# A two-layer kernel on one Trainium2 core: layer 0's start, with x staged in halves around w_out, one pass for bias and column sums, batch 1's statistics taken earlier, and chunk 0's last steps moved

## The reference, cut to what matters

```python
xs = in_proj_w @ gn(x)                       # 768 -> 1536 channels
xs = silu(depthwise_conv3x3(xs) + conv_b)
dt, Bs, Cs = split(x_proj_w @ xs)            # 48 + 4 + 4 rows
delta = softplus(dt_w @ dt + dt_b)
h[t] = exp(delta*A)*h[t-1] + delta*u*Bs      # scan over 4096 tokens, 4 states
y = sum_n(h*Cs) + D*u
y = layernorm(y over 1536 channels)*ln_g + ln_b
x = x + out_proj_w @ y                       # 1536 -> 768 channels
```

## Time and profile before

| what | value |
|---|---|
| time of the profiled execution | 3577.93 us |
| its span | 3576.1 us, so 1.8 us lie around it |
| median of three runs | 3577.36 us |
| busy shares of the span | TensorE 94%, VectorE 80%, ScalarE 67%, GpSimd 66% |
| VectorE busy in 60 to 80 us | 2.94 of 20 us |
| VectorE busy in 160 to 180 us | 12.46 of 20 us |
| VectorE busy in 220 to 240 us | 19.79 of 20 us |

### The profile page before, as it was taken

The page is one execution under the profiler, slowest core; times in us unless marked ns, Lnnn a source line. Parts: engine busy times, 40 slices in busy tenths (PEclk is TensorE's granted clock), DMA queues, the critical chain, the costliest instruction groups (busy, mean ns, idle before and its releaser), DMA issues. The chain is left out here.

```text
span 3576.1 us, 39074 instructions
## 1 busy us (share of the span) xinstructions
PE 3345.1 (94%) x10744; PEld 1719.7 (48%) x10744; DVE 2860.9 (80%) x4107; ACT 2378.3 (67%) x4143; POOL 2343.2 (66%) x1557
## 2 busy tenths in 40 slices
PE   6976899999999999999999999997989999999999
PEld 4522333434334343333434334342337877777887
DVE  4789999999999999999999999998733355655532
ACT  1477887888888878888888878886535555533211
POOL 0379999999999989999999999999800001122111
PEclk7887999999999999999999999998989999999999
DMA  7454455555655556555555555555532223366654
GB/s 278 138 172 105 129 155 141 148 153 144 163 136 160 140 151 162 141 152 141 148 159 148 151 141 149 150 141 163 126 111 77 65 86 107 124 202 213 212 189 156
DMA packets 218058, 529.91 MB, mean 148 GB/s; under 512 B 25624, under 2 KB 46808, under 8 KB 214896
## 3 DMA queue, kind: packets, MB, share of 16 engines
q1 hardware_dynamic: 174832, 376.39, 33.1%
q0 software_dynamic: 43008, 151.02, 19.3%
HBM read 346.17 MB, written 80.48 MB: 119 GB/s over the span
## 5 line engine op out<-in xcount | busy, mean ns | idle before, releaser
L516 PE MATMUL p_in<-xn,win_v 128*128 128x512 f32 (+1 forms) x2160 | 982.2, 603 | 74.4 <-ACT halo L762 46.9
L532 PE MATMUL p_op<-uy,wout_ring 128*128 128x512 f32 x2160 | 985.1, 605 | 29.5 <-DVE x_res L1014 29.4
L977 DVE TENSOR_TENSOR_SCAN p_da<-p_da,state,g_ring 128x512 f32<-128x512 f32 x672 | 827.2, 1276 | 69.0 <-ACT p_da L718 35.7
L949 POOL TENSOR_TENSOR g_ring<-du,bc 128x2048 f32<-128x2048 f32 x192 | 870.4, 4533 | 16.5 <-DMA bc<-bc_scratch 1.6
L1000 DVE SCALAR_TENSOR_TENSOR p_cv<-win_v,conv_w,p_cv 128x512 f32<-128x512 f32 x960 | 722.6, 753 | 51.8 <-ACT p_cv L820 30.9
L516 PEld LDWEIGHTS p_in<-xn,win_v 128*128 128x128 f32 x2160 | 406.2, 193 | 613.9 <-issue 613.4
L532 PEld LDWEIGHTS p_op<-uy,wout_ring 128*128 128x128 f32 x2160 | 402.1, 192 | 601.3 <-issue 545.3
L718 ACT ACTIVATE p_da<-delta,A 128x512 f32<-128x512 f32 x768 | 499.5, 682 | 12.5 <-ACT state L723 0.2
L983 DVE TENSOR_TENSOR g_ring<-p_da,bc 128x512 f32<-128x512 f32 x768 | 486.8, 675 | 0.0
L1457 PE MATMUL banks<-x_split,w_split 128*128 128x512 f32 x1152 | 459.7, 399 | 12.0 <-DVE x_split L1660 5.8
L1459 PE MATMUL banks<-x_split,w_split 128*128 128x512 f32 x1152 | 451.6, 392 | 0.0
(11 more groups left out here) (243 smaller groups left out, 4161.1 us busy)
## 6 DMA issues: line engine op xcount, KB each, us to landing
g_ring<-g_ring POOLq DMA_DIRECT2D x192, 512.0 KB, 5.0
win_v<-in_win SPq DMA_DIRECT2D x192, 384.0 KB, 3.1
wout_ring<-wout_scratch SPq DMA_DIRECT2D x184, 384.0 KB, 3.8
x_ring<-x_scratch SPq DMA_DIRECT2D x192, 256.0 KB, 2.7
q_scratch<-q_ring POOLq DMA_DIRECT2D x96, 256.0 KB, 2.5
x_split<-q_scratch SPq DMA_DIRECT2D x96, 256.0 KB, 3.3
out<-x_ring POOLq DMA_DIRECT2D x96, 256.0 KB, 2.9
x_res<-in_x SPq DMA_DIRECT2D x90, 256.0 KB, 3.8
```

The costliest lines, as they stand in the source:

```text
L516: last = nc.tensor.matmul(bank_in(i)[:, 0:n], WR[:, i % NW, t, :], XN[:, t, off:off + n], start=(t == 0), stop=(t == XT - 1))
L532: last = nc.tensor.matmul(p_op[:], OR[:, e % NO, k - h * HALF, :], ucol(c * K + k), start=(k == 0), stop=(k == K - 1))
L949: nc.gpsimd.tensor_tensor(G[:, i % NG], DU[:].unsqueeze(1).broadcast_to([P, NS, N]), BB[:], ALU.mult).then_inc(s_dbu, 1)
L977: nc.vector.tensor_tensor_scan(bank, bank, G[:, i % NG, n, :], init, ALU.mult, ALU.add)\
```

## The change

1. SyncE loads x of batch 0 in twelve halves (n = 0 to 11) of 1 MB, four of them ahead of w_out; `statistics(n)` follows with four `bn_stats` each.
2. The stationary side of the column sums is now two columns (ln_g/1536 and ln_b), 24 matmuls of 384 columns for sums and bias together; ScalarE copies the two rows out (`sq`), and 2 matmuls spread the one row over the 128 partitions and 6 turn the other to a column. All 36 one-column bias products of the start and the 36 of slots 1 to 3 go.
3. Batch 1's statistics are taken in halves too (n = 12 to 23). Seven of them (12 to 18) and the centring of k = 0 to 4 stand between the group norm and slot 2; in slots 2 to 11 two pieces each, and k = 5 to 11 in slots 2 to 8. Their loads go into `delta`, `bc` and `uy`, in SyncE's queue, behind statistics' own counts and among the loads of weights.
4. Chunk 0's last steps: ScalarE's `load_norm(1)` stands first in slot 12 and in six pieces, and tile 12's in_proj waits piece by piece; SiLU of the third four tiles stands ahead of tile 12's products with its table loaded ahead; `x_proj` part 2 stands between pieces 2 and 3 of tile 14's in_proj; the two copies to `x_dbl` stand ahead of and just behind tile 13's L820.

The core of the diff (`wait_ge` counts that only follow from it left out):

```diff
-                for t in range(1, XT):
-                    wait(sp, s_st, NB * (t - 3))
-                    sp.dma_start(stage0(t)..., XTR[0, :, t, :]).then_inc(s_xs[t % 4], 16)
+                def load_stage(n):
+                    if n >= 4:
+                        sp.wait_ge(s_st, NBH * (n - 3))
+                    sp.dma_start(stage(n)..., XTR[b, :, t, h * (T // 2):(h + 1) * (T // 2)])
...
+                for n in range(4):
+                    load_stage(n)
                 sp.dma_start(WT, g["wout"]).then_inc(s_wol, 16)
...
+                for n in range(2 * XT, 2 * XT + 4):
+                    load_stage(n)
                 for S in range(SLOTS):
-                    load_win(S + NW - 1)
+                    if S > 0:
+                        load_win(S + NW - 1)
+                    for n in range(2 * XT + 4, 4 * XT):
+                        if S == LOADED[n]:
+                            load_stage(n)
...
+LOADED = {16: 0, 17: 0, 18: 1, 19: 1, 20: 2, 21: 3, 22: 3, 23: 5}
...
# TensorE
-                        last = nc.tensor.matmul(p_da[:, h, 0:H2], lngd[:, k:k + 1].broadcast_to([P, P]),
-                                                WT[:, k, h * H2:(h + 1) * H2], ...)
-                bias_products(range(XT - len(S_BM)))
+                        last = nc.tensor.matmul(p_da[0:2, h, 0:H2], lncol[:, :, k], WT[:, k, h * H2:(h + 1) * H2], ...)
+                pe.wait_ge(s_lv, 3)
+                for h in range(2):
+                    nc.tensor.matmul(p_da[:, h, 0:H2], ident0[0:2, 0:1].broadcast_to([2, P]), SQ[0:2, h, 0:H2], ...)
+                for m in range(XT):
+                    last = nc.tensor.matmul(p_dt[:, 1, m:m + 1], SQ[0:2, h, o:o + P], ident0[0:2, 1:2], ...)
...
# ScalarE
+                    if S == K:
+                        load_norm(1)
...
+                    if S == S_XP[2] + 1:
+                        x_dbl_sums(0)
                     ... (L820 of tile S - 2)
+                    if S == S_XP[2]:
+                        nc.scalar.preload_act_table_set(SILUSET)
+                        silu(2)
+                    if S == S_XP[2] + 1:
+                        x_dbl(0)
...
# VectorE
                 norm0_vector(0, 0, 0)
+                vec.wait_ge(s_opl, PM)
+                nc.vector.tensor_copy(bm[:], p_dt[:, 1, 0:XT]).then_inc(s_set, 1)
+                centre(0)
+                centre(1)
+                for n in range(2 * XT, AHEAD):
+                    statistics(n, range(NBH))
+                    if n < 2 * XT + 3:
+                        centre(n - 2 * XT + 2)
                 for S in range(SLOTS):
-                    for n in (2 * S - 2, 2 * S - 1):
-                        if 0 <= n < NPIECE:
-                            nc.vector.bn_stats(stats1[:, n, :], stage(n)).then_inc(s_st, 1)
+                    if 2 <= S < 12:
+                        r = NBH * (AHEAD - 2 * XT) + 2 * (S - 2)
+                        statistics(2 * XT + r // NBH, range(r % NBH, r % NBH + 2))
+                        centre(S + 3)
```

More of the change, by code:

```diff
@@ L24 @@
 SPSET = "softplus"
+SILUSET = "silu_and_others"
 def wait(eng, sem, value):
@@ L296, in layer0 @@
         NPIECE = CPB * XT
+        NBH = NB // 2
+        AHEAD = 19
+        LOADED = {16: 0, 17: 0, 18: 1, 19: 1, 20: 2, 21: 3, 22: 3, 23: 5}
         S_NORM1 = NPIECE // 2 + 1
         def stage(n):
[L300 to L306, removed]
+            if n < 2 * XT:
+                n = n if n < 9 else n - 9
+                return (UY[:, 4 * n:4 * n + 4, :] if n < 4 else XRAW[:, 4 * n - 16:4 * n - 12, :] if n < 7 else
+                        BC[:, 4 * n - 28:4 * n - 24, :])
+            return (DL[:, 0:4, :], BC[:, 0:4, :], BC[:, 4:8, :], UY[:, 12:16, :])[n % 4]
         def bank_in(i):
@@ L450, in _ @@
                         wait(sp, s_dbu, K * c)
+                        if c == 0:
+                            sp.wait_ge(s_st, 2 * NPIECE)
                         sp.dma_start(BB[:].rearrange("p n t -> p (n t)"),
@@ L500, in first_row, with x_proj @@
                     last.then_inc(s_row, 1)
+                def x_proj(c, q, S):
+                    pe.wait_ge(s_silu, 3 * c + q + 1)
+                    wait(pe, s_delta, K * c)
+                    wait(pe, s_rstd, norms_before(S))
+                    for k in range(4 * q, 4 * q + 4):
+                        h = k % 2
+                        last = nc.tensor.matmul(p_dt[64 * h:64 * h + 64, 0, :], xpt[:, k, :], ucol(c * K + k),
+                                                start=(k < 2), stop=(k >= K - 2))
+                        if k >= K - 2:
+                            last.then_inc(s_xp, 1)
                 def in_proj(i, fold_of, pair_of, S):
@@ L511, in in_proj @@
                     for t in range(XT):
+                        if i == K:
+                            pe.wait_ge(s_xn, XT + t + 1)
+                        if t == 3 and S == S_XP[2]:
+                            x_proj(0, 2, S)
                         if t == 1 and fold_of is not None:
@@ L657, in _ @@
                         c = chunk_at(S, S_XP[q])
[L658 to L668, removed]
+                        if c is not None and (c, q) != (0, 2):
+                            x_proj(c, q, S)
                     if new is not None and S % K == 0:
@@ L836, in _ @@
                     c = chunk_at(S, S_XP[2] + 1)
-                    if c is not None:
-                        act.wait_ge(s_xp, 2 * (c + 1))
-                        wait(act, s_bw, 16 * c)
-                        nc.scalar.activation(XD[:], p_dt[:, 0, :], ACT.Copy).then_inc(s_xe, 1)
+                    if c is not None and c > 0:
+                        x_dbl_sums(c)
                     if i is not None:
@@ L846, in _ @@
                     c = chunk_at(S, S_XP[2] + 1)
-                    if c is not None:
-                        act.wait_ge(s_xf, c + 1)
-                        nc.scalar.activation(XD[:], p_dt[:, 1, :], ACT.Copy).then_inc(s_xd, 1)
-                    if S % K == 0 and S < NT:
+                    if c is not None and c > 0:
+                        x_dbl(c)
+                    if S % K == 0 and S < NT and S != K:
                         load_norm(S // K)
@@ L1016, in residual_add, with statistics, centre @@
                                                    accum_out=sum1[:, bb, m * CPB + k:m * CPB + k + 1]).then_inc(s_ov, 1)
+                def statistics(n, qs):
+                    vec.wait_ge(s_xs[n % 4], 16 * (n // 4 + 1))
+                    for q in qs:
+                        nc.vector.bn_stats(stats1[:, NBH * (n % (2 * XT)) + q, :], stage(n)[:, q, :]).then_inc(s_st, 1)
+                def centre(k):
+                    if k >= K:
+                        return
+                    for h in range(2):
+                        o = WT[:, k, h * H2:(h + 1) * H2]
+                        nc.vector.scalar_tensor_tensor(o, o, lng[:, k:k + 1], p_da[:, h, 0:H2],
+                                                       ALU.mult, ALU.subtract).then_inc(s_set, 1)
                 nc.vector.memset(xpt[:], 0.0).then_inc(s_set, 1)
```

145 lines of the change are left out of this document (72 added, 73 removed).

## The result

The changed kernel took 3554.86 us, the median of four runs (3552.52 to 3556.95); the kernel before took 3574.94 in the runs beside it. The ratio is 0.994, 95% interval 0.9927 to 0.9952: faster, by about 20 us or 0.6%, inside the forecast range, and about 9 us short of the forecast of 3545.7. The forecast's gain was 32.2 us. By the medians 20.1 of them came. By the two profiled executions it is 23.9 (3577.93 - 3554.01): the first profile of the kernel before, from which the forecast was counted, was 3.0 us slower than the median of 3574.94. The span of the profiled execution is 3551.9 us instead of 3576.1.

What follows compares the result with a forecast made beforehand. VectorE bounds the steady slots, so gains before slot 25 reach the end one for one. 2.4 - 0.4 + 11.2 + 2.2 + 8.7 + 2.0 + 6.1 = 32.2 us off 3577.9 gives 3545.7; range 3536 to 3560.

Steps and rivals of the forecast that it cites:

- signs that I had named for being wrong: gbi waiting for L604 or L608, statistics for DMA, in_proj for win_v, or another pace behind slot 25.
- A: Start up to gbi: 2.4 us gained, bounds 0 and 4.9; column sums cost nothing.
- rival 1: Column sums run at 1.2 GHz, up to 34.6 us, group norm about 8 us late: 3554, chance 0.22.
- B: From gbi to tile 0's first tap: VectorE's work 24.6 us against 24.2 before, 0.4 us lost.
- C: Slots 2 to 8: 6.85 us per slot, 41.8 instead of 53.0, 11.2 us gained, bounds 5 and 12.
- rival 2: Loads crowd out weights of tiles 4 and 5 in a full queue, in_proj late: 8 us, 3554, chance 0.18.
- D: Slots 8 to 12: 25.9 us instead of 28.1, 2.2 us gained, bounds 0 to 4.
- E: Slot 12 to 13: 5.5 us instead of 14.2, 8.7 us gained, bounds 6 to 9.
- F: Slot 13 to the first scan, 32.0 us before: 2.0 us gained, bounds -2 to 5.
- G: Slots 17 to 25 without statistics pieces: 96.1 us instead of 102.2, 6.1 us gained, bounds 4 and 8.
- Rivals 3 and 4: Chunk 0's TensorE clock at 0.50: 3619, chance 0.03; something else holds slots 2 to 16: 3569, 0.05, extreme 0.02.

Runs made afterwards that it cites:

- e7: Changed kernel with w_out asked for ahead of the first four halves of x: 3556.28 us.
- e1: Changed kernel with SyncE asking for the stores of w_out one per slot instead of five in slot 2: 3552.15 us.
- e8: Changed kernel with w_out's stores one per slot and x_proj's third part behind tile 14's whole in_proj, plus 12 one-column products in each of slots 1 to 3: 3557.02 us.
- e4: Changed kernel with load_norm(1), still in six pieces, back at the end of slot 12: 3557.12 us.
- e2: Changed kernel with x_proj's third part of chunk 0 behind all of tile 14's in_proj, not between its pieces: 3552.07 us.
- e3: Changed kernel with SiLU and its table load, both x_dbl copies and x_proj's third part moved back, load_norm(1) kept first in slot 12: 3553.64 us.
- e6: Changed kernel with two more bn_stats of 512 columns in each of slots 17 to 24: 3561.45 us.

## Why the prediction was right, and where its terms were off

**What bounds it: right.** The gain of the first 312 us arrives at the end. `bn_aggr` came 23.8 us earlier, every chunk's statistics of the layer norm from the second to the fourteenth 22.1 us earlier without change, the end of the span 24.2. That is one pair of profiles; in the second it is 20.0 at `bn_aggr` and 18.3 at the end. Of the signs that I had named for being wrong, one came: `in_proj` waited for `win_v`. The pace behind slot 25 was another too (49.07 us for the four slots instead of 47.34), but so it is in the second profile of the kernel before (50.25).

**A: right in kind, 1.2 us small.** The last statistics take 2.47 us instead of 4.85, as forecast. I let the last load land at 50.0; it landed at 48.87, within the bound I gave. Most of that 1.1 may be the four halves ahead of w_out (e7, 0.8). The column sums, rival 1, did not slow down (TensorE's timeline and a window):

```profile
24.79 17.11 PE L598 MATMUL p_da<-uy,x_dbl 128*2 128x384 f32 x48 [24.79 <-DMA uy<-in_wout]
42.79 1.55 PE L604 MATMUL p_da<-sq,ident 2*128 2x384 f32 x4 [0.89 <-ACT sq L705]
```

```profile
28.00:36.00 8.00, 8.00 (x27) 2.10 (x25) 5.31 (x9) 0.49 (x2) 0.00 (x0) 1.00 1.01 425
```

They began and ended within 0.4 us of where I put them (25.0, 42.3), at clock 1.00. By the rule of the Trainium skill, page "TensorE: Matmul & The Clock Gate", section on the HAM clock gate, that is what a busy engine gets; this row agrees with it, the one-column row of before does not.

**B: right.** 24.1 for 24.6, VectorE without a gap.

**C: the step that failed is the sum's price of nothing for late weights.** That was rival 2, and the half of its mechanism that came is the order: tile 4's weights stood behind 5 MB in SyncE's program in slot 2. They were asked for at 87.75, 5.8 us after tile 2's in_proj had ended, and landed 4.9 us later. The other half, that the bytes alone make them late, did not come (e1). I gave the rival 0.18 and 8 us; it was 4 us in this profile (e1 restores 41.8 exactly), up to 6 in others. I had worked out in the rival that the queue had no air there and then summed C as if it had. The pace of 6.85 itself, and the cause of the old pace, were right (e8).

**D: mis-sized, 0.5 for 2.2 (1.1 in e1, where slots 8 to 12 take 27.0).** I kept 7.6 us for the slot behind a SiLU; it took 8.6. ScalarE's way from the `p_cv` step ahead of a SiLU to the next one is the same as before, 8.70 us (137.11 to 145.81) and 8.69 (149.15 to 157.84). But VectorE's taps start only 0.93 us behind the first of the two steps instead of 1.97, since no centring stands in between any more, and there is none in the slot itself; so VectorE stands 2.71 us at the second instead of 0.63, and the microsecond of centring saved ahead of the SiLU is lost again behind it. Slot 12 took 7.4 for 6.7. In e1, with `load_norm(1)` as long (4.34 and 4.33 us), it took 6.8, so that 0.6 of it is again the late weights: in the changed kernel ScalarE waits 0.47 us for tile 11's in_proj ahead of `load_norm(1)`, in e1 it does not. The part behind the SiLU was read from the traces and not tried.

**E: right**, 8.5 for 8.7, but e4 shows that a part was given back: at slot 12 (1.7) and at the split (2.6).

**F: mis-sized, -0.3 for 2.0, and the placing of x_proj was priced wrongly.** In my own steps tile 11's last tap to `x_dbl` ready was to take 13.3 us; it took 15.2 (164.35 to 179.59). The adds and SiLU took the 2.8 and 1.9 I had, but I counted `x_proj` and the half in_proj behind it as full-clock work, 1.9 and 2.7 us, and they took 3.6 and 3.7; ScalarE's steps behind took 3.1 for 4.0. I missed that the clock falls while TensorE stands ahead of them, and that the same half could have filled that wait: 4.7 us together (e2), 2.6 of them the clock (e4). The moves of SiLU and `x_dbl` are worth 2.0 us (e3 against e2). That this is the forecast's figure is chance: the forecast's 2.0 was for all of F, with 2.7 put on for the half in_proj, and without it my steps gave these moves 3.9 (0.7 + 0.5 + 2.7). And 1.3 us of F depend on which profile of the kernel before is taken, 32.0 or 30.7. The first has `x_dbl`'s fold (L522) at 1.85 us, the second at 1.13.

**G: mis-sized, 4.1 for 6.1** (e6 gives the same price). I took the period of slots 25 to 29 for all; the slots behind two pairs of softplus take 13.9 each, where the reference had 13.3, and slot 23 took 12.1 for 11.5.

**Rivals 3 and 4** did not come: in_proj ran at 5.37 in slots 5 to 11, and C and E gained.

**The number.** No bound of the sum was broken, but five of its seven terms came out short. The time fell into the range because the range had room for the rivals, and lies outside the 3538 to 3551 that I gave the forecast itself.

## What to carry to other kernels

When loads for later use are moved forward into a queue, list what each urgent load now stands behind, in bytes and in the issuing engine's own blocking, and pace the bulky ones one per step. A wait in the middle of a run of matmuls costs twice: the rest of the run could have filled it, and what follows may run at half clock, as it did here behind waits of 3.4 and 3.95 us, and not behind those of 1.25 and 1.39; put the dependent product behind everything that needs nothing. And price the removal of work from a near-bound engine with the neighbour's chain in view: fourteen pieces of 0.61 us, 8.5 in all, were worth 4.1 us.

## What the hardware showed that I had not expected

With two columns on the stationary side and 384 on the moving one, the granted clock stayed at 1.00 (2.4 GHz); with 128 stationary columns and one moving, it fell to 0.50 (1.2 GHz) while TensorE stood busy without a gap, and the in_proj behind took 7.0 us. Issues of five stores of 384 KB, behind some 3 MB still in the queue (by my count of the loads not yet landed), held SyncE's queue for 10.79 us. And the same instructions of slot 27 took from 13.3 to 16.2 us in different profiles of the same program with the granted clock at 0.79 in the longer case and at 1.00 in the shorter.
